# One normalisation group more, shared lower parts, and threefold stack loads in a convolution-and-attention chain

## The reference, cut to what matters

```python
# layer 1: attention over all 256 positions of a batch, one head, q and k of width 8
scores = einsum('bnd,bmd->bnm', xt @ wq + bq, xt @ wk + bk) / sqrt(8)
x = x + (einsum('bnm,bmc->bnc', softmax(scores), xt @ wv + bv) @ wo + bo)
# layer 2: group norm (32 groups of 2 channels, over all positions), then
# neighborhood attention: 8 heads of width 8, a 7 x 7 window, a bias per head
h = gn(x)
scores = einsum('bnijd,bnijkd->bnijk', q / sqrt(8), gather(k)) + bias
x = x + einsum('bnijk,bnijkd->bnijd', softmax(scores), gather(v))
# then: self attention, routed feed-forward, gated attention, routed feed-forward
```

## Time and profile before

| what | value |
|---|---|
| median of 3 runs | 170.19 us (169.01 to 171.38) |
| the profiled execution's own time | 168.97 us |
| its span | 167.1 us |
| mean granted TensorE clock | 0.973 |

### The profile page before, as it was taken

The page is one execution under the profiler, slowest core; times in us unless marked ns, Lnnn a source line. Parts: engine busy times, 40 slices in busy tenths (PEclk is TensorE's granted clock), DMA queues, the critical chain, the costliest instruction groups (busy, mean ns, idle before and its releaser), DMA issues. The chain is left out here.

```text
span 167.1 us, 3148 instructions
## 1 busy us (share of the span) xinstructions
PE 146.9 (88%) x1087; PEld 102.9 (62%) x1087; DVE 111.3 (67%) x385; ACT 75.1 (45%) x197; POOL 50.8 (30%) x78
## 2 busy tenths in 40 slices
PE   7999977799999998799787999967999899899920
PEld 2598736598888886588234554445665637678620
DVE  2027664987879898536644538947969289696873
ACT  3445605335353545451636550397535433555140
POOL 7051359786555657110400023520002200000000
PEclk9999999999999999999999999999999959999985
DMA  5993044373450000058000000000000000000002
GB/s 147 358 417 99 4 127 93 96 201 110 129 132 2 6 0 4 0 117 329 15 0 0 0 0 0 2 0 0 6 0 0 4 0 0 0 0 4 0 0 65
DMA packets 7098, 10.30 MB, mean 62 GB/s; under 512 B 2719, under 2 KB 5608, under 8 KB 6698
## 3 DMA queue, kind: packets, MB, share of 16 engines
q1 hardware_dynamic: 6880, 9.72, 19.2%
q10 hardware_dynamic: 202, 0.38, 0.9%
HBM read 8.52 MB, written 1.57 MB: 60 GB/s over the span
## 5 line engine op out<-in xcount | busy, mean ns | idle before, releaser
L453 PE MATMUL bank<-onesb 128*128 128x512 bf16 x142 | 36.7, 406 | 1.1 <-DVE onesb L1221 1.1
L453 PEld LDWEIGHTS bank<-onesb 128*128 128x128 bf16 x142 | 14.0, 105 | 16.1 <-issue 3.5
L418 POOL TENSOR_TENSOR half_mem<-identb,nm 128x256 bf16<-128x256 bf16 x32 | 19.5, 614 | 11.5 <-DVE nm L1302 11.3
L1302 DVE TENSOR_REDUCE nm<-bank 128x2 bf16<-128x352 f32 x32 | 16.3, 516 | 4.0 <-PE bank L607 3.7
L1037 ACT ACTIVATE mid_mem<-mid_mem 128x352 f32<-128x352 f32 x20 | 9.8, 496 | 18.4 <-DVE mid_mem L1313 18.4
L625 PE MATMUL bank<-stack_mem 72*128 72x176 bf16 x64 | 13.7, 240 | 0.1
L631 PE MATMUL bank<-half_mem,onesb 128*128 128x176 bf16 x64 | 13.5, 239 | 0.0
L605 PE MATMUL bank<-stack_mem 72*128 72x176 bf16 x64 | 12.7, 241 | 0.9 <-DVE nm L1302 0.9
L607 PE MATMUL bank<-half_mem,identb 128*128 128x176 bf16 x64 | 12.6, 239 | 0.0
L1313 DVE TENSOR_TENSOR mid_mem<-bank,bias_mem 128x352 f32<-128x352 f32 x20 | 10.3, 542 | 0.0
L629 PE MATMUL bank<-bias_mem,identb 128*128 128x176 bf16 x72 | 9.3, 238 | 0.0
(11 more groups left out here) (279 smaller groups left out, 330.8 us busy)
## 6 DMA issues: line engine op xcount, KB each, us to landing
stack_mem<-qk_parts SPq DMA_DIRECT2D x21, 96.0 KB
bias_mem<-bias_q SPq DMA_DIRECT2D x1, 1408.0 KB, 8.2
bias_mem<-bias_k SPq DMA_DIRECT2D x1, 1408.0 KB, 11.7
mid_mem<-w SPq DMA_DIRECT2D x1, 1024.0 KB, 7.5
qk_parts<-half_mem SPq DMA_DIRECT2D x4, 192.0 KB, 2.7
qk_parts<-half_mem SPq DMA_DIRECT2D x4, 128.0 KB, 2.4
mid_mem<-w2b SPq DMA_DIRECT2D x1, 512.0 KB, 8.4
Cs<-cst SPq DMA_DIRECT2D x1, 336.0 KB, 4.3
```

The source lines that it names most:

```text
L418: pool.tensor_tensor(diag1[:, b % 2, h, :].rearrange("p (q k) -> p q k", q=TB), identb[:, :].unsqueeze(1).to_broadcast([P, TB, P]), nm1[:, ...
L453: pe.matmul(idle[:, :].rearrange("p (k q) -> p k q", k=4), onesb[:, :], onesb[:, :].unsqueeze(1).to_broadcast([P, 4, P]), start=True, stop ...
L1302: dve.tensor_reduce(nm1[:, n // NH, n % NH, :], bank[n % 2][:, 0:TB * SPAN].rearrange("p (q k) -> p q k", q=TB), AX.X, ALU.max, negate=Tru ...
```

## The change

Batch 1 gets a normalisation group of its own; batches 2 and 3 share the last one. The bias' middle part is cast by ACT instead of POOL. For batches 2 and 3 only the rest stays on DVE; ACT casts the middle part and POOL subtracts for the low part. The six constant tiles are set by DVE at its start. On PE, the eight warm-ups before the loop go, `project(1)` moves ahead of six others, and `max_scores` of heads 0 and 1 come ahead of the values product. Each stack side is read by one transfer with a source pattern of 3 x 24 rows instead of three transfers of 24 rows; of batches 0 and 1 SP loads the queries and ACT the keys, of 2 and 3 SP loads both, after the stores of both. Some semaphores are merged, which is left out below.

```diff
-WARM = {"update": 2, "group": 4, "scale": 6, "start": 9, "weights": 2, "stacks": 8, "b_norm": 12, "logits": 2, "loads": 4, "routing": 10,
+WARM = {"update": 1, "group": 4, "scale": 6, "start": 9, "weights": 2, "b_norm": 12, "logits": 2, "loads": 4, "routing": 10,
         "selection": 11, "c_norm": 34, "a_steps": {3: 4},
         "d_norm": 18, "d_norm_2": 2, "first_expert": 5, "slots": 9}
...
         def store_parts(queue, b, parts, at):
-            queue.wait_ge(sem("qk_part"), 2 * b + parts - 1)
+            if b < 2:
+                queue.wait_ge(sem("qk_part"), 2 * b + parts - 1)
+            else:
+                queue.wait_ge(sem("middle_part" if parts == 2 else "low_part"), b - 1)
             queue.dma_start(qk_parts[b, at:at + parts].rearrange("i r n -> r i n"), part[:, 0:parts, b * N:b * N + N]) \
                 .then_inc(sem(f"parts_stored{b}"), 16)
 
-        def load_stack(queue, b, pieces):
+        def load_stack(queue, b, kind):
 
             queue.wait_ge(sem(f"parts_stored{b}"), 2 * 16)
-            for kind, piece in pieces:
-                side, stack = (0, QS) if kind == "queries" else (1, KSt)
-                first = 0 if kind == "queries" else piece
-                stack = stack[3 * HD * piece:3 * HD * piece + 3 * HD]
-                rows = qk_parts[b, first:first + 3].rearrange("i (d s h) n -> s (i d) (h n)", d=HD, s=2)[side]
-                queue.dma_start(stack[:, b, :, :].rearrange("r h n -> r (h n)"), rows) \
-                    .then_inc(sem(f"stack_landed{b}"), 16)
+            side, stack = (0, QS) if kind == "queries" else (1, KSt)
+            rows = qk_parts[b].rearrange("i (d s h) n -> s (i d) (h n)", d=HD, s=2)[side]
+            (stride, _), inner = rows.ap
+            step = 0 if kind == "queries" else HD * stride
+            threefold = bass.AP(tensor=rows.tensor, offset=rows.offset, ap=[[step, 3], [stride, 3 * HD], list(inner)])
+            queue.dma_start(stack[:, b, :, :].rearrange("r h n -> r (h n)"), threefold) \
+                .then_inc(sem(f"stack_landed{b}"), 16)
...
 
             store_parts(sp, 0, 2, 3)
             store_parts(sp, 0, 3, 0)
-            load_stack(sp, 0, [("keys", 1), ("queries", 0), ("queries", 1)])
-            for b in range(1, B):
+            load_stack(sp, 0, "queries")
+            store_parts(sp, 1, 2, 3)
+            store_parts(sp, 1, 3, 0)
+            load_stack(sp, 1, "queries")
+            for b in range(2, B):
                 store_parts(sp, b, 2, 3)
                 store_parts(sp, b, 3, 0)
-                load_stack(sp, b, [(kind, piece) for piece in range(3) for kind in ("queries", "keys")])
+            for b in range(2, B):
+                load_stack(sp, b, "keys")
+                load_stack(sp, b, "queries")
...
             pool.wait_ge(sem("pool_const"), 9)
             some_heads = slice(PE_HEADS[0], NH, PE_HEADS[1] - PE_HEADS[0])
             pool.tensor_copy(bias_part[:, 0, :, :], biasK[:, some_heads, :]).then_inc(sem("bias_part"), 1)
-            pool.wait_ge(sem("qk_part"), 2)
             pool.wait_ge(sem("bias_part"), 1)
             pool.tensor_tensor(bias_rest[:, :, :], biasK[:, some_heads, :], bias_part[:, 0, :, :], ALU.subtract) \
                 .then_inc(sem("bias_part"), 1)
 
-            group_scale(1, slice(1, B), gn_g[:, 2 * B + 1:3 * B])
-            pool.wait_ge(sem("bias_part"), 2)
-            pool.tensor_copy(bias_part[:, 1, :, :], bias_rest[:, :, :]).then_inc(sem("bias_part"), 1)
+            group_scale(1, slice(1, 2), gn_g[:, 5:6])
+            group_scale(2, slice(2, B), gn_g[:, 10:12])
             pool.wait_ge(sem("bias_part"), 3)
             pool.tensor_tensor(bias_part[:, 2, :, :], bias_rest[:, :, :], bias_part[:, 1, :, :], ALU.subtract) \
                 .then_inc(sem("bias_part"), 1)
-            for k, (tile, value) in enumerate([
-                    (XN["a"][:, :, C:C1], 1.0), (XF["a"][C:P, :], 1.0),
-                    (XF["b"][C:C1, :], 1.0),
-                    (mean2[C:C1, :], 1.0), (ones4[:, :], 1.0), (loads1[:, :], float(N))]):
-                if k:
-                    pool.wait_ge(sem("later_const"), k)
-                pool.memset(tile, value).then_inc(sem("later_const"), 1)
-            pool.tensor_copy(prefixb[:, :], Cs[:, CST["prefix"]]).then_inc(sem("later_const"), 1)
+            for b in range(2, B):
+                c = slice(b * N, b * N + N)
+                pool.wait_ge(sem("middle_part"), b - 1)
+                pool.tensor_tensor(part[:, 2, c], qkr[:, c], part[:, 1, c], ALU.subtract).then_inc(sem("low_part"), 1)
+            pool.tensor_copy(prefixb[:, :], Cs[:, CST["prefix"]]).then_inc(sem("pool_late"), 1)
...
             turn_x1(1)
             turn_x1(2)
             attend0(3)
+            pair(1, 1, 1)
             keep_warm(WARM["update"], bank[7])
             turn_x1(3)
             keep_warm(WARM["group"], bank[7])
-            pair(1, 1, 3)
+            pair(2, 2, 2)
+            project(1)
             keep_warm(WARM["scale"], bank[7])
-            project(1)
             project(2)
             project(3)
-            for t in range(T):
-                last = pe.matmul(bank[7][:, t * C:t * C + C], XN1[:, t * P:t * P + P], W0s[:, W0["wv1"]],
-                                 start=True, stop=True)
-            last.then_inc(sem("v1_p"), 1)
+
+            def values1():
+                for t in range(T):
+                    last = pe.matmul(bank[7][:, t * C:t * C + C], XN1[:, t * P:t * P + P], W0s[:, W0["wv1"]],
+                                     start=True, stop=True)
+                last.then_inc(sem("v1_p"), 1)
 
             def max_scores(b, h):
 
                 n = b * NH + h
-                if n == 0:
-                    keep_warm(WARM["stacks"], bank[0])
                 if h == 0:
-                    pe.wait_ge(sem(f"stack_landed{b}"), 6 * 16)
+                    pe.wait_ge(sem(f"stack_landed{b}"), 2 * 16)
                     if b == 0:
                         pe.wait_ge(sem("pool_const"), 9)
                 if n >= 2:
@@ -663,8 +667,10 @@
                                             CT1[:, b % 2, g * N + q * P:g * N + q * P + P], ident)
                 last.then_inc(sem("turn1"), 1)
 
-            for n in range(AHEAD):
+            for n in range(AHEAD - 1):
                 max_scores(n // NH, n % NH)
+            values1()
+            max_scores(0, AHEAD - 1)
...
             def normed0(b):
-                act.wait_ge(sem("gn_nb"), min(b, 1) + 1)
+                act.wait_ge(sem("gn_nb"), min(b, 2) + 1)
                 act.activation(XN1[0:C, b * N:b * N + N], bank[b][0:C, 0:N], ACT.Identity,
                                bias=gn_nb[:, b:b + 1], scale=gn_r[:, b:b + 1]).then_inc(sem("xn1"), 1)
...
             exp0(3)
             high_part(0)
             turned_p0(3)
-            load_stack(act, 0, [("keys", 0), ("keys", 2), ("queries", 2)])
+            act.wait_ge(sem("bias_part"), 2)
+            act.activation(bias_part[:, 1, :, :], bias_rest[:, :, :], ACT.Copy).then_inc(sem("bias_part"), 1)
+            load_stack(act, 0, "keys")
             normed0(1)
+            high_part(1)
             normed0(3)
-            for b in range(1, B):
+            for b in range(2, B):
                 high_part(b)
+            for b in range(2, B):
+                c = slice(b * N, b * N + N)
+                act.wait_ge(sem("qk_rest"), b + 1)
+                act.activation(part[:, 1, c], qkr[:, c], ACT.Copy).then_inc(sem("middle_part"), 1)
+            load_stack(act, 1, "keys")
             act.wait_ge(sem("v1_p"), 1)
             act.activation(V1[:, :, :, 0:HD],
                            bank[7][:, :].rearrange("p (t h d) -> p t h d", t=T, h=NH), ACT.Copy).then_inc(sem("v1"), 1)
-            act.wait_ge(sem("wa_landed"), 16)
-            act.wait_ge(sem("wg_landed"), 16)
+            act.wait_ge(sem("wa_landed"), 32)
...
             dve.memset(onesb[:, :], 1.0).then_inc(sem("onesb"), 1)
             dve.wait_ge(sem("onesb"), 1)
             dve.tensor_copy(onesf[:, :], onesb[:, :]).then_inc(sem("onesb"), 1)
-            dve.wait_ge(sem("wvo"), 1)
+            for tile, value in [(XN["a"][:, :, C:C1], 1.0), (XF["a"][C:P, :], 1.0), (XF["b"][C:C1, :], 1.0),
+                                (mean2[C:C1, :], 1.0), (ones4[:, :], 1.0), (loads1[:, :], float(N))]:
+                dve.memset(tile, value).then_inc(sem("later_const"), 1)
+            dve.wait_ge(sem("weights_p"), 2)
             dve.tensor_copy(Wvo[:, :], bank[7][0:C1, 0:C]).then_inc(sem("wvo_s"), 1)
...
-            def lower_parts(b):
+            def rest(b):
                 c = slice(b * N, b * N + N)
                 dve.wait_ge(sem("part_high"), b + 1)
                 dve.tensor_tensor(qkr[:, c], bank[QK_BANK[b]][:, 0:N], part[:, 0, c], ALU.subtract) \
                     .then_inc(sem("qk_rest"), 1)
+
+            def lower_parts(b):
+                c = slice(b * N, b * N + N)
                 dve.wait_ge(sem("qk_rest"), b + 1)
```

(47 more changed lines are left out.)

## The result

| | before | after |
|---|---|---|
| median of 4 runs each, same chip | 170.22 us | **180.91 us** (180.02 to 181.90) |
| ratio after/before, 95% interval | | 1.063 (1.054 to 1.072) |
| the profiled execution: time, span | 168.97, 167.1 us | 180.92, 179.1 us |

The change is slower by 10.7 us. The forecast was 176.9, +6.7; the range of 171 to 187 holds the result. (The profiled execution of experiment 10 took 180.82 us where its four others took 171.0 to 174.1, so its trace is not read.)

A forecast was written before the change was run, and what follows sets the result against it. PE, busy 88%, bounds the kernel; at the head loop's start PE's warm-ups and DVE's queue end together. First maxima move from 32.66 to 39.3, +6.7; 170.19 + 6.7 = 176.9 us, range 171 to 187.

The forecast's parts named there:

- The number of engines and the packet: Stack loads: each threefold transfer runs on 3 DMA engines at 0.16 us per 4 KB packet; forecast's chance 0.62.
- rival B: Stack loads: three engines, but packets no faster than today's 0.29 us; 183 to 200 us, chance 0.15.
- Rival A: Stack loads: transfers spread over 12 engines as now, so not slower; +1.1, 171.3 us, chance 0.17.
- The time of a stack: Stack loads: 144 rows on 3 engines are 48 packets each, 7.7 us per stack against 3.5.
- data to 32.4, complete S = 33.1: Stack 0: issued 23.8, first packet 0.9 later, data to 32.4; S, when PE has the stack, is 33.1.
- in time, barely: Stacks 2 and 3 in the head loop: complete at 53.1 and 60.8, against 53.3 and 62.0 needed.
- The order of the gates: Head loop's start: the gate copies follow the values, and line 1297, waiting for the third, stands ahead of the first maxima.
- S + 4.5: First maxima on DVE: S plus two heads 0.65, values 1.89, then 0.1, gate copies 1.4 and 0.45; 37.6 us.
- Rival C: Head loop's start: 12 engines, and the gate copies don't hold the maxima; −2.4, 167.8 us, chance 0.06.
- The clock: PE after idling until S: 3.4 us at half speed, +1.7, which puts the first maxima at 39.3.
- Store 1: Store of batch 1's parts: its cast, slowed by POOL's subtraction, ends at 28.8, so issue at 28.8 instead of 29.53.
- The parts costed at nothing: Shared casts and subtractions, middle bias on ACT, memsets on DVE: no cost; bias copy up to 2 us without ACT's cover.

The follow-up runs named there:

- experiment 10: Kernel of run 9 with POOL's last bias subtraction moved between the two last groups' scales: 174.06 us (171.04 to 180.82).
- run 4: After kernel with the two outer levels of the load's source pattern swapped, 24 x 3 rows instead of 3 x 24: 172.84 us, ratio 1.013.
- run 7: Kernel of run 4 with two more warm-ups at "update" (three in all) and eleven behind the value products: 170.74 us, ratio 1.002.
- Run 12: After kernel, threefold loads kept, with "update" at 3, 24 warm-ups ahead of the wait for stack 0 and 11 behind the value products: 182.69 us, ratio 1.071.
- run 9: Kernel of run 5 with "update" at 3, two warm-ups more ahead of the transposes of batch 3: 169.22 us, ratio 0.994.
- run 5: Kernel of run 4 with ACT's three small gate copies moved ahead of its load of stack 0: 170.64 us, ratio 0.998.
- runs 3: After kernel with the small subtraction that waits for the third gate copy moved behind the first three maxima: 182.95 us, ratio 1.072.
- run 11: Kernel of run 9 with POOL's bias subtraction between the last group scales and SP waiting for stack 1 before stores 2 and 3: 173.98 us.
- run 1: After kernel with its stacks read by six loads of 24 rows again: 173.95 us, ratio 1.018.
- run 6: Kernel before with only its loads changed, to one transfer of 24 x 3 rows per side: 170.02 us, ratio 1.001.

## Why the prediction was right in kind and 4 us short

**The number of engines and the packet: right.** Three small packets per load, a share of 0.20, 82 GB/s and 159 ns per 4 KB packet are the predicted 3, 0.19, about 75 GB/s and 0.16; rival B, three engines at 0.29 us per packet, falls by the last of them. The rule of the Trainium skill's "DMA: Bandwidth & Descriptors", section "Why a DMA increments its semaphore by 16 and not by 1", holds here also for the keys, whose leading 3 has a stride; run 4 changes only the order of the pattern's levels and gets 12 engines. Rival A falls by it. It would have been right for the swapped pattern: A's 171.3 against 172.84 measured, and 170.74 in run 7 where the clock isn't low.

**The time of a stack: too short.** This is one step that failed, "data to 32.4, complete S = 33.1". The stores of batch 0 and the issue came 0.3 us later than said, the first packet 1.6 us behind the issue (0.9 said; issuing a load of 72 rows took 0.82 us by itself), and the rows took 25.68 to 34.78, 9.1 us instead of 7.7. The stores of batch 1 are not the reason, though they had to pass the same three engines: they were issued at 29.75, and the time was lost before. The packets of 25.6 to 29.5:

```profile
DMA packets 45, 0.18 MB, mean 47 GB/s; under 512 B 0, under 2 KB 0, under 8 KB 45
```

Fifteen rows per engine took 3.8 us, since two rows on each took 0.87 to 0.97 us instead of 0.16, the first and one at 27.3 to 27.4. From 29.52 to 34.78 all 99 others took 159 ns each. What held the six rows stays open. Complete: 35.25, 2.15 late. Stacks 1 and 2 took 10.35 and 10.74 us from issue to completion, where 9.3 and 8.5 stood in the sum. Only from stack 2's completion to stack 3's, with issue, first packet and stores out of the way, was it the 7.7 us (57.99 to 65.69). So "in time, barely" was wrong for stack 2: complete at 57.99, not 53.1. Run 12 shows that this alone gives +11.5 at head 16. "In time" held for stack 1 by luck: it was complete at 46.34 instead of 43.1, later than the 44.5 at which it was said to be needed, and PE did not wait only because the low clock had put its first head off to 48.9. In run 12, at full clock up to there, PE waits 1.51 us for it.

**The order of the gates: right.** S + 4.5 was 0.65 + 1.89 + 0.1 + 1.4 + 0.45. Run 12, at full clock, has 34.93 for S and 39.34 for the maxima: 4.4. Rival C, in which the copies hold nothing, falls by the 10.02 us of idle DVE ahead of line 1323.

**The clock: right in kind, too small.** The forecast gave one low stretch of 3.4 us at a price of 1.7. From 35.30 to 41.85 the after kernel took 6.55 us where run 12 took 4.4, so 2.1 up to there; but the level stayed at 0.50 until 46.8, PE having waited 4.72 us ahead of 35.30 and 2.41 more ahead of 42.44, and heads 2 to 5 cost 1.9 more (+9.2 to +11.1). A whole low stretch was not foreseen: 23.0 to 29.8, after PE had waited 0.83 us at 22.06 with one warm-up ahead; the kernel before had two there, waited 0.54, and stayed at 1.00. The diff takes that warm-up away ("update" 2 to 1), and I gave it no term; the low stretch delays projections 1 to 3. Where the stacks are in time, its price is 1.4 us (run 9 against 5, which differ in two warm-ups there and nothing else), and together with the second stretch 2.1 us (run 7 against 4).

**Store 1: wrong.** It was issued at 29.75, not at 28.8 (29.53 before). The cast met POOL as predicted (28.21, 1.50 us, beside 27.39 to 29.57), but started 1.2 us later than said. Batch 1's projection began at 25.75 instead of 24.9, behind ACT's issue of a load (24.10, 0.81 us) and its normalisation, and took 1.22 us at the low clock. The clock is the smaller part of this: in run 7, where it is high, the cast starts at 27.90 and store 1 is issued at 29.20. Batch 1's own normalisation gained nothing in the after kernel and 0.3 us there. The parts costed at nothing (shared parts, memsets, the bias) leave no trace in the sum: run 7 has them all and differs from before by the 1.75 us of the gate order at the first heads, and by less than its interval in time.

**How it adds up.** Read off the traces, the forecast was +6.7 and the kernel came to +12.0. The 5.3 between them are 2.15 for stack 0, 0.4 for the clock up to the first maxima, 1.9 for heads 2 to 5, and 0.8 for the wait for stack 2. By experiment, the 10.7 us of the medians are 8.1 for the leading 3 (after to run 4) and 2.1 to 2.2 for the low clock and the gate copies behind the stack, which either run 5 or run 7 takes back alone; the 0.4 left is within the scatter. They do not simply add, since two things reach about +11 in the loop by different ways: head 15 stands at +11.1 by the late start and the slow heads, and head 16 at +12.1 by stack 2. That is why taking away the one (runs 3 and 12) gave nothing: their medians (182.95 and 182.69) lie above that of the after kernel, and each has one more low stretch at PE's wait for stack 2.

## What to carry to other kernels

Merging transfers is a change of the access pattern, so look at what stands outermost: a leading 3 put 144 rows of 4 KB on three engines, the same rows with 24 outermost ran on twelve, and the difference was 8 us of 181. A transfer that gets slower also delays the next store and load behind it on the same engines, so follow the whole chain of stacks and not just the first. And when work moves behind a wait, follow the small operations that stand in program order between it and the critical engine: three copies of 1 us together held all maxima, and moving them into idle time won 3 us at the first head. Idle time on one engine is not free for its neighbours, though: POOL's subtraction, moved into a gap of POOL, held a tiny operation of DVE for 2.2 us (run 11).

## What was not expected

- The same 144 rows took 332 ns per packet as six loads (run 1) and 173 ns as two loads with 24 outermost (run 4), both on 12 engines with both queues active: 5.1 us of packets against 2.8. I had read the 0.29 us of before as something the 12 engines share. The number of transfers is part of it but not all: in the kernel before, the same swap brings 298 ns down only to 205 and 3.5 us to 3.0 (run 6), and six loads took 3.5 us there and 5.1 in run 1. Why was not tried.
- A wait of PE of 0.83 us, with one warm-up fewer ahead of it, was followed by 6.8 us at 0.50 (also in runs 4 and 5); two more warm-ups there (run 9) left none.
- Issuing four stores took SP 5.39 us (from 36.76) while stack 1's rows held the three engines, and 3.03 in run 4 with those rows on twelve; two stores before that took 0.88 in both.
